# A gated network prepares its following stage in small pieces and one to two batches sooner

## What is computed

```python
h = shift_token(x)                      # the second half of the channels comes from the token before
mu = h.mean(-1, keepdims=True); var = h.var(-1, keepdims=True)
h = (h - mu) / jnp.sqrt(var + 1e-05) * lg + lb
h = h @ w1 + b1                         # 256 -> 2 * 682
a, g = jnp.split(h, 2, axis=-1)
h = a * jax.nn.gelu(g, approximate=False)
x = x + h @ w2 + b2                     # 682 -> 256
```

## Time and profile before

| | before |
|---|---|
| time, median of 3 runs | 4137.27 us (4133.03 to 4146.78) |
| the profiled execution's own time | 4133.88 us |
| its span, first to last instruction | 4132.2 us |
| TensorE busy | 3681.5 us, 89% of the span |
| VectorE busy | 2371.7 us, 57% |
| ScalarE busy | 1791.8 us, 43% |
| GpSimd busy | 1668.0 us, 40% |
| mean granted TensorE clock | 0.947 of full speed |

### The profile page before, as it was taken

The page is one execution under the profiler, slowest core; times in us unless marked ns, Lnnn a source line. Parts: engine busy times, 40 slices in busy tenths (PEclk is TensorE's granted clock), DMA queues, the critical chain, the costliest instruction groups (busy, mean ns, idle before and its releaser), DMA issues. The chain is left out here.

```text
span 4132.2 us, 60613 instructions
## 1 busy us (share of the span) xinstructions
PE 3681.5 (89%) x17520; PEld 2213.3 (54%) x17520; DVE 2371.7 (57%) x6484; ACT 1791.8 (43%) x4090; POOL 1668.0 (40%) x1891
## 2 busy tenths in 40 slices
PE   6999999999869999899899989868999999758995
PEld 3556555665535555555455555533555555445664
DVE  6676777677556564233566633425666666354556
ACT  2445454454425555211455542114555555303444
POOL 2343334343356665100676642431222221165664
PEclk8999999999889999999999999988999999958997
DMA  6655665566211111345011121122222222038993
GB/s 104 73 74 68 93 83 78 66 94 80 54 54 36 41 51 38 143 179 205 16 51 51 36 74 56 54 68 74 67 59 58 68 58 53 19 135 288 318 304 133
DMA packets 223891, 377.22 MB, mean 91 GB/s; under 512 B 39180, under 2 KB 155344, under 8 KB 217264
## 3 DMA queue, kind: packets, MB, share of 16 engines
q1 hardware_dynamic: 207776, 350.99, 36.0%
q0 software_dynamic: 6480, 17.77, 1.1%
q10 hardware_dynamic: 9408, 5.78, 0.5%
HBM read 169.64 MB, written 84.74 MB: 62 GB/s over the span
## 5 line engine op out<-in xcount | busy, mean ns | idle before, releaser
L758 DVE CUSTOM_DVE_ANT_0 a_ps<-a_ps,a_mask 128x128 f32<-128x128 f32 (+3 forms) x1024 | 479.6, 513 | 196.7 <-PE a_ps L513 179.0
L368 POOL TENSOR_SCALAR_AFFINE_SELECT a_probs_c<-a_probs_c 128x256 f32<-128x256 f32 (+1 forms) x384 | 187.3, 504 | 668.7 <-ACT a_probs_c L663 668.3
L2505 ACT ACTIVATE c_probsT<-c_ps 128x512 f32<-128x512 f32 x512 | 298.6, 601 | 327.6 <-PE c_ps L2327 318.4
L2644 DVE TENSOR_REDUCE c_neg_max<-c_ps 128x1 f32<-128x512 f32 x512 | 337.0, 683 | 151.1 <-PE c_ps L2315 149.7
L663 ACT ACTIVATE a_probs_c<-a_ps 128x512 f32<-128x512 f32 x640 | 344.9, 603 | 99.9 <-PE a_ps L531 70.7
L513 PE MATMUL a_ps<-a_packed_qk 65*128 65x128 f32 (+3 forms) x1024 | 339.4, 375 | 46.0 <-DVE a_maxima L758 26.9
L1101 POOL TENSOR_TENSOR w_probs<-w_probs,w_inv 128x1024 f32<-128x1024 f32 x128 | 242.3, 1893 | 334.6 <-DVE w_inv L1465 334.6
L549 PE MATMUL a_ps<-a_probs_c,a_v 128*64 128x512 f32 (+3 forms) x2048 | 318.6, 455 | 0.9 <-POOL a_probs_c L368 0.8
L531 PE MATMUL a_ps<-a_packed_qk 67*128 67x512 f32 (+3 forms) x1024 | 288.6, 345 | 2.2 <-DMA a_packed_qk<-a_max_half 2.1
L1356 ACT ACTIVATE w_probs<-w_ps_s,w_neg_max 128x256 f32<-128x256 f32 x512 | 235.9, 478 | 66.8 <-DVE w_neg_max L1460 66.1
L2315 PE MATMUL c_ps<-c_packed_qk 68*128 68x512 f32 x512 | 254.7, 503 | 11.2 <-DVE c_neg_max L2644 6.6
(11 more groups left out here) (355 smaller groups left out, 8052.1 us busy)
## 6 DMA issues: line engine op xcount, KB each, us to landing
a_packed_qk<-a_halves SPq DMA_DIRECT2D x512, 128.0 KB, 4.6
d_w<-in_L_ffn_second SPq DMA_DIRECT2D x71, 516.0 KB, 4.9
d_w<-in_L_ffn_first SPq DMA_DIRECT2D x71, 512.0 KB, 5.5
rows_dram<-f_zeros SPq DMA_DIRECT2D x8, 4128.0 KB, 16.1
c_packed_qk<-c_halves SPq DMA_DIRECT2D x256, 128.0 KB, 2.3
w_v<-w_v_next SPq DMA_DIRECT2D x16, 1024.0 KB, 4.7
d_rows<-rows_dram SPq DMA_DIRECT2D x71, 129.0 KB, 4.8
f_y_res<-y_dram SPq DMA_DIRECT2D x16, 512.0 KB, 3.9
```

The lines of the kernel that those rows point to most:

```text
L758: last = nc.vector.tensor_tensor_reduce(tile, tile, mask[:, (NT - 1 - i) * P:], 1.0, -3e38, ALU.add, ALU.max, accum_out=maxima_of[:, hd // ...
L2505: nc.scalar.activation(probsT[:, q % 2, r, :], ps_again[u % 2][:, :], ACT.Exp).then_inc(exp_done.sem, 1)
L2644: nc.vector.tensor_reduce(neg_max[:, g % 2, 0, s % GS:s % GS + 1], bank("s", s)[:, :], AX.X, ALU.max, negate=True).then_inc(max_ready.sem, 1)
```

## The change

In `gated_ffn`, for whichever stage follows:

- GpSimd calls `ahead_fill` in each of the batches 0 to 5, right behind the inverse roots for the next batch, instead of once in batch 5. In the diffusion attention it now takes a part number: 16 fills of one head each are dealt over the six calls as 2, 3, 3, 2, 3, 3; the last call also does `ones`, `v` in four pieces instead of one, and `neg_half`.
- SyncE issues the following stage's loads in batch 5, behind the loads of `shifted` for batch 6, instead of at the end of batch 7.
- VectorE does the following stage's `ahead_vector` in batch 6 behind chunk 2, instead of in batch 7 behind chunk 2.

The code is shared, so the first gated network changes too: its SyncE issues the local attention's loads in batch 5. Its `ahead_fill` and `ahead_vector` are empty.

```diff
--- before.py
+++ after.py
@@ -25,7 +25,7 @@
         self.nc, self.name, self.side = nc, name, side
         self.ctx = ExitStack()
         self.ctx.semaphores = []
-        self.ahead_sync = self.ahead_vector = self.ahead_gpsimd = self.ahead_fill = lambda eng: None
+        self.ahead_sync = self.ahead_vector = self.ahead_gpsimd = self.ahead_fill = lambda eng, part=0: None
 
     def sb(self, name, shape, dt=fp32):
         return self.ctx.enter_context(self.nc.sbuf_tensor(self.name + name, shape, dt, side=self.side))
@@ -1641,6 +1641,8 @@
                     sp.wait_ge(hn_ready.sem, hn_ready.at(b, 1))
                     load(sp, b + 1)
                 clear(b)
+                if b == B - 3:
+                    following.ahead_sync(sp)
                 if LAST and b >= 1:
                     store(b - 1)
                     sp.dma_start(x_res[:, :, :], x_v[b]).then_inc(x_res_in.sem, 16)
@@ -1651,7 +1653,6 @@
                     sp.dma_start(y_res[:, :, :], y_v[b + 1]).then_inc(y_res_in.sem, 16)
             if cleared is not None:
                 sp.dma_start(cleared[B * B * N:, :], zeros[:, 0:D + 2]).then_inc(zeros_out.sem, 16)
-            following.ahead_sync(sp)
             store(B - 1)
             if cleared is not None:
                 sp.wait_ge(zeros_out.sem, 16 * (B + 1))
@@ -1677,11 +1678,11 @@
                     norm_output(b - 1)
                 if b + 1 < B:
                     roots_in.step(pool, b + 1, 0, rstd[:, :], mv[:, :, 1], EPS, neg_half[:, :])
-                if b + 3 == B:
-                    if LAST:
+                if b < B - 2:
+                    if LAST and b >= 1:
                         pool.wait_ge(y_ready.sem, y_ready.at(b - 1, 1))
                     pool.wait_ge(roots_in.ready.sem, roots_in.ready.at(b + 1, 1))
-                    following.ahead_fill(pool)
+                    following.ahead_fill(pool, b)
             if LAST:
                 pool.wait_ge(y_ready.sem, y_ready.at(B - 2, 1))
             following.ahead_gpsimd(pool)
@@ -1816,7 +1817,7 @@
                         nc.vector.tensor_tensor(y_res[:, :, :], y_res[:, :, :],
                                                 b2[:, :].unsqueeze(1).to_broadcast([P, NT, D]), ALU.add)\
                           .then_inc(biased.sem, 1)
-                    if c == 2 and b + 1 == B:
+                    if c == 2 and b + 2 == B:
                         following.ahead_vector(dve)
                 add_output(b)
             if LAST:
@@ -1919,6 +1920,7 @@
     x_loaded, stats_linked, in_order = signal("x_loaded", 16), signal("stats_linked"), signal("in_order", 5)
     hn_ready, kept, hT_psum = signal("hn_ready"), signal("kept"), signal("hT_psum", KD)
     passed_pool, passed_dve = signal("passed_pool", 0), signal("passed_dve", 0)
+    filled = signal("filled")
     roots_in = InverseRoots(ctx, nc, "c_roots_in", 1)
 
     first = []
@@ -1979,13 +1981,21 @@
                                            ALU.subtract, ALU.mult)
         last.then_inc(hn_ready.sem, 1)
 
-    def ahead_fill(pool):
-        nc.gpsimd.memset(packed_qk[2 * ROWS:3 * ROWS, :, :, :].bitcast(fp32), 1.0).then_inc(made_pool.sem, 1)
-        pool.wait_ge(made_pool.sem, 1)
-        nc.gpsimd.memset(ones[:, :], 1.0)
-        nc.gpsimd.memset(v[:, :, :, :], 0.0).then_inc(made_pool.sem, 1)
-        pool.wait_ge(made_pool.sem, 2)
-        nc.gpsimd.memset(v[:, :, :, DH:DH + 1], 1.0)
+
+    FILLS = 6
+
+    def ahead_fill(pool, part):
+        heads = range(part * H // FILLS, (part + 1) * H // FILLS)
+        for hd in heads:
+            nc.gpsimd.memset(packed_qk[2 * ROWS:3 * ROWS, :, hd, :].bitcast(fp32), 1.0).then_inc(filled.sem, 1)
+        pool.wait_ge(filled.sem, (part + 1) * H // FILLS)
+        if part < FILLS - 1:
+            return
+        nc.gpsimd.memset(ones[:, :], 1.0).then_inc(made_pool.sem, 1)
+        for t in range(NT):
+            nc.gpsimd.memset(v[:, t, :, :], 0.0).then_inc(filled.sem, 1)
+        pool.wait_ge(filled.sem, H + NT)
+        nc.gpsimd.memset(v[:, :, :, DH:DH + 1], 1.0).then_inc(made_pool.sem, 1)
         nc.gpsimd.memset(neg_half[:, :], -0.5).then_inc(made_pool.sem, 1)
         pool.wait_ge(made_pool.sem, 3)
```

## The result

| | before | after |
|---|---|---|
| time, median of 6 runs each | 4144.30 us (4133.03 to 4156.11) | 4114.07 us (4107.56 to 4118.12) |
| the profiled execution's own time | 4133.88 us | 4107.56 us |
| its span | 4132.2 us | 4105.7 us |
| second gated network, first transposes to last product | 282.7 us | 254.9 us |

After over before is 0.9927, with an interval of 0.9906 to 0.9948: faster by 0.7%. The median lies in the predicted range and 8 us above the predicted 4106; three more runs of before have moved its own median up by 7.

What follows compares the result with a forecast made beforehand. TensorE was taken to bound the second gated network; -19.0 - 16.1 + 5.5 + 0.2 = -29.4 us gave 4104.5 from the profiled execution, 4107.9 from the median. Predicted 4106 us, 0.75% faster, range 4099 to 4116.

Steps and rivals of the forecast that it cites:

- second stall: Batch 7, second gated network: VectorE waits in `ahead_vector` for late loads; issuing them in batch 5 removes it, -19.0 us.
- first stall: Batch 5, second gated network: `f_hn` held up by GpSimd's long fills of `packed_qk` and `v`; its removal gives -16.1 us.
- small collisions: Batches 1 to 5, second gated network: short fills delay `f_hn` and so TensorE's transposes; +5.5 us, bounds 4.6 and 6.6.
- `ahead_vector` in batch 6: VectorE's work for the next stage may wait for GpSimd's residual addition; +0.2 us, between nothing and 2.35.
- The rule: Each `f_hn` instruction lets one whole fill pass: 3m + 0.48 us with three fills, 2m + 0.48 + 0.34 with two.
- m: Time of one fill of 1024 elements in a partition, taken as 0.93 us, between 0.86 and 0.99.
- The loads: 28 loads issued in batch 5 behind those of `shifted`: they don't slow `shifted`, cost 0.
- The first gated network: Its SyncE issues seven loads in batch 5 behind the bulk store; none of its waits is for them, 0.
- Short fills: Rival: short fills don't hold up `f_hn`, so the 5.5 falls away; -34.9 us, 4099 to 4102, chance 0.10.
- The clock: Rival: TensorE's clock falls at each small stall in the second gated network; -19.9 us, 4114 to 4117, chance 0.07.
- The early loads: Rival: the early loads hurt, making `shifted` of batch 6 late; -14.8 us, 4119 to 4122, chance 0.05.
- The forecast's own range: Range of the forecast as summed, all terms between their bounds plus 1 us for spread: 4102 to 4112, chance 0.73.

Runs made afterwards that it cites:

- early_only: Kernel before with the following stage's loads in batch 5 and `ahead_vector` in batch 6, fill in one piece; 4121.82 us, ratio 0.9953.
- loads_only: Kernel before with only the loads moved to batch 5, `ahead_vector` still in batch 7, fill in one piece; 4120.44 us, ratio 0.9955.
- fill_behind_hn: Changed kernel with GpSimd's fills held back until VectorE has written `f_hn` for the next batch; 4105.64 us, ratio 0.9915.
- fills_only: Kernel before with only the fills cut and dealt over six batches, loads and `ahead_vector` still in batch 7; 4135.90 us, ratio 0.9979.

## Why the prediction was right, and where a size was off

| term | predicted | measured | from |
|---|---|---|---|
| second stall | -19.0 | -18.9 | 60.16 to 41.28; the same in `early_only`, 41.23 in `loads_only` |
| first stall | -16.1 | -16.1 | 44.87 and 32.23 (rows of before) against twice 30.51 |
| small collisions | +5.5 (4.6 to 6.6) | +7.1 | 7.1 in `fill_behind_hn` against the change |
| `ahead_vector` in batch 6 | +0.2 | +0.06 | 30.58 against 30.57, 41.28 against 41.23, without it in `fills_only` and `loads_only` |
| sum | -29.4 | -27.8 | stage 282.7 to 254.9 |

**The stalls.** Both were what the rows of before said, and the two halves of the change taken alone gave each its own. The second was a matter of the loads alone.

**The small collisions: the mis-sized term.** The rule was right, one whole fill for each VectorE instruction, as many as there are. The sizes were low in two places. First m: I took 0.93 us for a fill and 0.99 as its upper bound, from rows in which nothing comes between fills. With an `f_hn` between them three fills take 3.02 us, 1.01 each; undisturbed, in `fill_behind_hn`, 2.72, 0.91 each. Two `f_hn` are let in between three fills, and each pushes the fill behind it back by 0.15 us (2 x 0.15 is the 0.30; between two fills it is one, 1.98 for 1.84). `f_hn` is then 3.02 and 0.55, where I had 2.79 and 0.48: 3.57 for 3.27, and 2.86 for 2.68. The pauses sum to 6.06, 0.5 over the forecast. Second, I took a pause for its whole price. It costs 0.16 to 0.23 us more: groups of matmuls that follow one another start 1.72 us apart though each takes 1.88, an overlap of 0.16 that a pause takes away, and the transposes behind it take 1.09 for 1.04. Five times that is the other 1.0 us.

**`ahead_vector`.** `c_q_scale` was held until GpSimd's addition ended (2684.24 + 1.66 is 2685.90, and 2683.52 + 2.35 is 2685.87), as the upper bound of this term supposed, and TensorE lost next to nothing: the transposes at 2689.44 have no pause. That was close, and partly luck. The prediction asked only whether the product of chunk 3 could wait. But GpSimd's first instruction for `f_rstd` took 1.00 us instead of 0.23 beside this work, so `f_hn` ended at 2689.38, 0.06 us before the transposes, where a batch leaves 0.8 with nothing in the way (2623.30 and 2624.12 in batch 4 before); by these rows a slightly longer `ahead_vector` would have made a pause of its own.

The Trainium skill, "SBUF — State Buffer", section "Who interferes with whom", says so of this pair: the statistics use VectorE's own port and pass, the scaling takes the shared pair and waits. The trace agrees: 1.39 us for the statistics and 0.38 for their aggregation, as in the other batches, and 1.66 for a scaling of 4 elements in a partition that takes 0.17 in `fills_only`.

**The loads.** `shifted` was waited for 2.03 us in batch 5 instead of 1.53, but 1.91 in batch 3, which has no loads behind it; no stall came of either. The first gated network took 255.3 us from its first transposes to its last product, and 255.2 before.

**The rivals.** Short fills do hold `f_hn` up (3.57). The clock doesn't fall at a pause of 1.7 us (1.00 in the windows, transposes at 1.09; behind 14.19 they took 1.97). The early loads don't hurt. The forecast's own range, 4102 to 4112, was left by 2 us: 1.6 for the collisions, and the median of before is itself uncertain by more, 4137 with three runs and 4144 with six.

## What to carry to other kernels

Cutting a long GpSimd instruction bounds how long VectorE can be held, at one piece for each of its instructions, so cut finer than VectorE's own count there, and leave the pieces in one batch: spreading them repeats the collision. Better by the stage's length, 247.8 us against 250.0, is to start them behind the VectorE instructions that TensorE waits for, with one wait on a semaphore that exists already. And look for the same pair of rows elsewhere, above all at a program's start, where here nothing else hid it; expect the wait that it hid, a load or a queue on another engine, to show up next.

## What the runs showed of the hardware

- VectorE's `tensor_scalar` instructions and GpSimd's fills take turns, instruction by instruction. Four `f_hn` beside 16 fills waited for four of them (4.29 us), beside three for three (3.57), beside one for one (3.85, with the fill at 2.65). GpSimd pays too: a fill with an `f_hn` let in before it takes 1.09 us instead of 0.94.
- The delay goes both ways. GpSimd's first instruction for `f_rstd`, 0.23 us in the other batches, took 1.00 at 2685.84, beside VectorE's last two small scalings and its copy `c_wqk` of 0.67 us at 2686.07; it ended 0.10 behind the copy.
- Not every VectorE instruction meets the fills: the bias at 2659.39, with both inputs in SBUF, took its usual 1.21 us in the middle of the fills of `v`, which only write. Beside a GpSimd instruction that reads, the power at 2719.21 in stage `c`'s first normalisation, the bias again took 1.22, and the power 2.11 where such a one takes 1.04. The Trainium skill, "SBUF — State Buffer", section "Who interferes with whom", says that a VectorE instruction with two SBUF inputs contends with a GpSimd instruction that reads SBUF, not with one that only writes it, and the trace agrees.
